# An attention kernel's normalised input: turned through DRAM and VectorE instead of TensorE, with a reordered opening

## What is computed

```python
x_norm = (x - mu) / jnp.sqrt(var + EPS) * gamma + beta
q = x_norm @ qkv[:, :KEY]
k = x_norm @ qkv[:, KEY:2 * KEY]
v = x_norm @ qkv[:, 2 * KEY:]
scores = jnp.einsum('bsk,btk->bst', q, k) * scale
scores = jnp.where(causal[None], scores, -jnp.inf)
out = jax.nn.softmax(scores, axis=-1) @ v
out = out @ o_proj
x1 = _layernorm(x + out + x)
...
h = jax.nn.silu(x1 @ w1.T); h = jax.nn.silu(h @ w3.T); h = h @ w2.T
out = out.at[indices_k[:, k]].add(gates[:, k:k + 1] * h)
```

## Time and profile before

| | |
|---|---|
| three runs | 1683.23, 1684.08, 1684.34 us (median 1684.08) |
| profiled execution, its time | 1682.32 us |
| span in the profile | 1680.3 us |
| granted TensorE clock, mean | 1.00 |
| TensorE busy (PE) | 98% of the span |
| VectorE (DVE), ScalarE (ACT), GpSimd (POOL) busy | 49%, 40%, 17% |
| DMA | 92.58 MB, mean 55 GB/s |

### The profile page before, as it was taken

How to read it: one execution, slowest core, us unless ns; L and a number is a source line. 1 busy time by engine, 2 the same in 40 slices (tenths; PEclk the granted TensorE clock), 3 DMA queues, 4 the chain that set the end, 5 groups by cost and what they waited for, 6 DMA issues and landing times.

```text
span 1680.3 us, 23574 instructions
## 1 busy us (share of the span) xinstructions
PE 1650.4 (98%) x7923; PEld 1369.7 (82%) x7923; DVE 828.1 (49%) x2168; ACT 671.6 (40%) x1301; POOL 282.6 (17%) x491
## 2 busy tenths in 40 slices
PE   7999999999999999999999999999999999999998
PEld 5888888878888888788888888888878888888886
DVE  5454434454453445455343456443456556555563
ACT  5443333443342334343322445332344444444443
POOL 1120201111120111121110112010122212212121
PEclk9999999999999999999999999999999999999999
DMA  4111201121111011121101132111154223132200
GB/s 157 57 51 51 70 32 38 64 71 63 70 51 51 32 50 64 58 101 49 53 19 38 45 100 95 38 57 45 63 115 74 36 39 50 25 50 43 32 0 7
DMA packets 173764, 92.58 MB, mean 55 GB/s; under 512 B 137296, under 2 KB 137296, under 8 KB 173664
## 3 DMA queue, kind: packets, MB, share of 16 engines
q1 hardware_dynamic: 162768, 72.41, 15.8%
q10 hardware_dynamic: 10896, 18.90, 3.6%
HBM read 57.71 MB, written 33.57 MB: 54 GB/s over the span
## 4 chain that ended last, share of the span: by engine, by line
PE 79%; issue 13%; POOL 3%; ACT 3%; DVE 2%; DMA 1%; SPq 0%; ACTq 0%; POOLq 0%; DVEq 0%
PE psum L334 24%; PE psum L336 24%; PE psum L335 24%; PE psum L1221 3%; PE psum L1159 1%; POOL rstd L454 1%; PE psum L1326 1%; PE psum L1325 1%; PE psum L1318 1%; PE psum L1317 1%; ACT xin L580 1%; ACT tok L580 1%; POOL expo L529 1%; ACT affine L564 0%; DVE stats L823 0%
## 5 line engine op out<-in xcount | busy, mean ns | idle before, releaser
L334 PE MATMUL psum<-xt_hi,g_hi 128*128 128x512 f32 (+3 forms) x640 | 239.5, 374 | 0.4 <-DVE g_lo L849 0.4
L628 ACT ACTIVATE pt_hi<-psum 128x512 fp32r<-128x512 f32 (+3 forms) x160 | 84.8, 530 | 369.6 <-PE psum L1221 363.7
L336 PE MATMUL psum<-xt_lo,g_hi 128*128 128x512 f32 (+3 forms) x640 | 230.0, 359 | 0.0
L335 PE MATMUL psum<-xt_hi,g_lo 128*128 128x512 f32 (+3 forms) x640 | 229.2, 358 | 0.0
L334 PE MATMUL psum<-v_hi,pt_hi 128*128 128x512 f32 x544 | 222.8, 410 | 1.8 <-DVE pt_lo L859 1.4
L336 PE MATMUL psum<-v_lo,pt_hi 128*128 128x512 f32 x544 | 213.1, 392 | 0.0
L335 PE MATMUL psum<-v_hi,pt_lo 128*128 128x512 f32 x544 | 212.8, 391 | 0.0
L451 POOL TENSOR_TENSOR var_eps<-meanvar,eps 128x2 f32<-128x2 f32 (+1 forms) x97 | 19.3, 199 | 1048.8 <-DVE meanvar L827 1046.7
L864 DVE TENSOR_REDUCE rowmax<-psum 128x1 f32<-128x512 f32 (+3 forms) x160 | 97.5, 610 | 197.7 <-PE psum L336 197.2
L746 ACT ACTIVATE act_f<-psum 128x512 f32<-128x512 f32 x128 | 76.5, 598 | 210.0 <-PE psum L336 210.0
L529 POOL TENSOR_TENSOR expo<-euler,shifted 128x32 f32<-128x32 f32 x16 | 86.9, 5430 | 298.0 <-DVE shifted L1061 298.0
(11 more groups left out here) (145 smaller groups left out, 3401.7 us busy)
## 6 DMA issues: line engine op xcount, KB each, us to landing
xin<-in_x ACTq DMA_DIRECT2D x64, 256.0 KB, 2.8
tok<-in_x SPq DMA_DIRECT2D x64, 256.0 KB, 2.6
x_scratch<-tok SPq DMA_DIRECT2D x64, 256.0 KB, 2.0
out_dram<-tok SPq DMA_DIRECT2D x64, 256.0 KB, 2.0
x_in<-x_scratch SPq DMA_DIRECT2D x64, 256.0 KB, 4.2
xin<-in_w_t ACTq DMA_DIRECT2D x8, 256.0 KB, 2.8
w_sb<-in_w_t SPq DMA_DIRECT2D x1, 1024.0 KB, 5.2
raw<-in_wq_t SPq DMA_DIRECT2D x1, 768.0 KB, 6.1
```

Source lines behind the costliest of these rows:

```text
L334: pe.matmul(o, ws, ms, start=first, stop=False, skip_group_check=True)
L335: pe.matmul(o, w_lo, ms, start=False, stop=False, skip_group_check=True)
L336: return pe.matmul(o, ws, m_lo_, start=False, stop=last, skip_group_check=True)
L628: act.activation(pt_hi[:, n % 2, 0:w], psum[:, turn_bank(turn_use(t, c)), 0:w], ACT.Copy).then_inc(pt_hi_ready, 1)
```

## The change

For all groups but the first of batch 0, TensorE no longer turns the input. SP stores each normalised pair of tiles in DRAM (`xn_scratch`) and reads a group back with quadrants exchanged (`load_xq`: 16 DMAs of 64 KB) into the place of `xt_lo`; VectorE transposes it in 32x32 blocks into the place of `xt_hi` (`turn_x`, four instructions of 128x512); ScalarE applies gamma and beta back into the place of `xt_lo` (`affine_x`); VectorE splits it there (`split_x`, now one feature chunk of all four tiles of the group, where a unit was two chunks of two tiles). Transposes of group g+1 stand in tile k = 1, with the statistics of a pair moved there from k = 0; splits 0 to 3 in tile k = 2. For group 0 of the next batch transposes and splits 0 and 1 stand at the end of tile 14, splits 2 and 3 in tile 15, which also gets a pair's statistics. SP, not ScalarE, now loads `xin`. Since a split covers all four tiles, the first `project_v` of a group waits for all four splits.

In the opening, TensorE runs 14 matmuls on a constant, starts the fold before the first turn, and leaves the last block of the second fold to the end; pairs 2 to 4 of batch 0 have buffers of their own.

```diff
+            def store_xn(b, pair, first=False):
+                sp.wait_ge(x_normed, b * PAIRS + pair + 1)
+                sp.dma_start(pair_rows(xn_scratch, b, pair), x_pair(pair, first)).then_inc(xn_stored, DMA)
+            def load_xq(b, g):
+                rows_of = xn_scratch[bass.ds(b * S + g * (GROUP * P), GROUP * P), :].rearrange("(t j) (c q i) -> q j c t i", j=LANES, q=QUADRANTS, i=LANES)
+                for c in range(DC):
+                    for q in range(QUADRANTS):
+                        sp.dma_start(xt_b[q * LANES:(q + 1) * LANES, c, columns(g)].rearrange("j (t i) -> j t i", i=LANES),
+                                     rows_of[q][:, c]).then_inc(xq_loaded[g % 2], DMA)
...
+                if t == TILES - 1 and not last:
+                    sp.wait_ge(scores_ready, b * CHUNKS + BEFORE[t] + 1)
+                    load_xq(b + 1, 0)
...
+            def affine_x(b, g, c):
+                act.wait_ge(xq_turned, (b * GROUPS + g - 1) * DC + c + 1)
+                act.activation(xt_b[:, c, columns(g)], xt_a[:, c, columns(g)],
+                               ACT.Identity, bias=beta_sb[:, c:c + 1], scale=gamma_sb[:, c:c + 1]).then_inc(affine_ready, 1)
...
+            def turn_x(b, g, c):
+                dve.wait_ge(xq_loaded[g % 2], (2 * b + (g + 1) // 2) * DC * LOADS)
+                dve.transpose(xt_a[:, c, columns(g)], xt_b[:, c, columns(g)]).then_inc(xq_turned, 1)
...
-                if more and k == 0:
+                if more and k == 1:
+                    for c in range(DC):
+                        turn_x(b, g + 1, c)
+                if more and k == 2:
+                    split_x(b, g + 1, 0)
                     split_x(b, g + 1, 1)
-                if more and k == 2:
-                    split_x(b, g + 1, 2)
...
+                if t == TILES - 2 and not last:
+                    for c in range(DC):
+                        turn_x(b + 1, 0, c)
+                    split_x(b + 1, 0, 0)
+                    split_x(b + 1, 0, 1)
                 if more and k == 2:
+                    split_x(b, g + 1, 2)
                     split_x(b, g + 1, 3)
                     split_v(b, GROUP * (g + 1))
                     split_g(b, g + 1)
...
+                if more and k == 1:
+                    affine_x(b, g + 1, 0)
+                    affine_x(b, g + 1, 1)
...
+                if tile % GROUP == 0 and tile:
+                    pe.wait_ge(xt_ready, 1 + (b * GROUPS + tile // GROUP + 1) * XUNITS)
...
-                if more and k == 2:
-                    turn_x(b, g + 1, 2)
-                if t == TILES - 2 and not last:
-                    turn_x(b + 1, 0, 0)
-                if t == TILES - 1 and not last:
-                    turn_x(b + 1, 0, 2)
...
+            for _ in range(WARMING):
+                pe.matmul(psum[:, XBANK, 0:P], ident[:], ident[:], start=True, stop=True)
+            fold_weights(0, 0, (0, 1))
+            turn_x(0)
+            fold_weights(0, 0, (2, 3))
+            turn_x(1)
+            for c in range(1, DC):
+                fold_weights(0, c, range(DC))
+            for c in range(2):
+                fold_weights(1, c, range(DC - 1))
+            turn_x(2)
+            for c in range(2, DC):
+                fold_weights(1, c, range(DC - 1))
+            turn_x(3)
+            for c in range(DC):
+                fold_weights(1, c, (DC - 1,))
```

More of the change, by code:

```diff
@@ L346, in load_x1, with x_pair, pair_rows, stored @@
                                  rows_of[q]).then_inc(x1_loaded[slot], DMA)
+        def x_pair(n, first):
+            if first and n in EARLY:
+                return xt_a[:, n - 1, 2 * GROUP * P:4 * GROUP * P].rearrange("p (s d) -> p s d", s=2)
+            return xin[:]
+        def pair_rows(dram, b, pair):
+            return dram[bass.ds(b * S + 2 * pair * P, 2 * P), :].rearrange("(s p) d -> p s d", p=P)
+        def stored(b, pair):
+            return (b * PAIRS + pair - 1) * DMA
+        def second_half(g):
+            return 2 * (g + 2) + 1
+        def first_half(g):
+            return 2 * (g + 3)
+        def ahead(b, pair, last):
+            if pair < PAIRS:
+                return b, pair
+            return None if last else (b + 1, pair - PAIRS)
+        def columns(g):
+            return slice(GROUP * g * P, GROUP * (g + 1) * P)
         block = whole.enter_context(nc.Block())
@@ L390, in tile @@
                     store_out(b - 1, TILES + t - 3)
-            for t in range(3):
-                tile(0, t, before=False)
+                if normed:
+                    sp.wait_ge(xn_stored, stored(*normed))
+                    to_load = ahead(b, first_half(g) if k else second_half(g), last)
+                    if to_load:
+                        load_x(*to_load)
+                if k == GROUP - 1:
+                    if g + 2 < GROUPS:
+                        sp.wait_ge(scores_ready, b * CHUNKS + 1)
+                        load_xq(b, g + 2)
+                    elif g + 2 > GROUPS and not last:
+                        sp.wait_ge(scores_ready, b * CHUNKS + BEFORE[t] + 2)
+                        load_xq(b + 1, g + 2 - GROUPS)
+            for t in range(2):
+                tile(0, t, before=False)
+            for n in EARLY[0:2]:
+                store_xn(0, n, first=True)
+            sp.wait_ge(xn_stored, stored(0, EARLY[1]))
+            load_xq(0, 1)
+            store_xn(0, EARLY[2], first=True)
+            tile(0, 2, before=False)
             with sp.Fori(0, B - 1) as b:
@@ L476, in tile @@
                 pool.tensor_tensor(y, y, y, ALU.add).then_inc(res_doubled, 1)
[L477 to L480, removed]
+                if k == GROUP - 1 and ahead(b, first_half(g), last):
+                    norm_x(*ahead(b, first_half(g), last))
                 if t:
@@ L484, in tile @@
                     norm_behind(b - 1, TILES - 1)
[L485 to L490 removed]
+                if t == 0 and not before:
+                    norm_x(b, EARLY[2])
+                if k == 1 and ahead(b, second_half(g), last):
+                    norm_x(*ahead(b, second_half(g), last))
             def batch(b, last):
@@ L497, in batch @@
                         tile(b + 1, t)
-            for pair in range(FIRST_PAIRS):
+            for pair in range(FIRST_PAIRS - 1):
                 norm_x(0, pair)
@@ L828, in statistics, with norm_x @@
                 done.then_inc(requested, 1)
[L830 to L839, removed]
+            def norm_x(b, pair, first=False):
+                if first and pair in EARLY:
+                    dve.wait_ge(x_early_loaded[pair - EARLY[0]], DMA)
+                else:
+                    dve.wait_ge(x_loaded, (pair + 1) * DMA if first else (b * PAIRS + pair - 2) * DMA)
+                if not first or pair:
+                    dve.wait_ge(x_normed, b * PAIRS + pair)
+                y = x_pair(pair, first)
+                statistics(lambda s: y[:, s - 2, :], 2, 4, x_variance)
@@ L934, in tile @@
                     split_v(b, t + 1)
-                if t == TILES - 2 and not last:
-                    split_x(b + 1, 0, 1)
                 if t == TILES - 1 and not last:
@@ L959, in tile @@
                         split_v(b, GROUP * (g + 1) + j)
-                if more and k == 0:
-                    norm_x(b, 2 * (g + 1) + 1)
-                if t == TILES - 2 and not last:
-                    norm_x(b + 1, 1)
+                if t == 0 and not before:
+                    norm_x(b, EARLY[2], first=True)
+                if k == 1 and ahead(b, second_half(g), last):
+                    norm_x(*ahead(b, second_half(g), last))
                 from_tile = TILES - 1 - GROUP
```

216 lines of the change are left out of this document (105 added, 111 removed).

## The result

The changed kernel takes 1714.71 us (median of 4 runs, 1712.17 to 1717.38) against 1683.78 us before (1683.23 to 1684.34): ratio 1.018, interval 1.0168 to 1.0192. It is 30.9 us slower; 12 were forecast, and the time lies 4.7 us above the upper end of the range. The profiled execution took 1712.17 us, its span 1710.4, 30.1 above the span before.

A forecast was written before the change was run, and what follows sets the result against it. TensorE, busy 98%, was taken as the bound, with VectorE's list order deciding its waits. 29.6 + 4.5 - 14.4 - 24.4 - 4.8 - 2.2 = -11.7 gave 1694.0 us profiled, 1696 against the median; range 1685 to 1710.

The forecast's parts named there:

- What is taken away: TensorE, main stage: 60 units of four transposes go at 0.44 us each; with the turns' waits, 29.6 us gained.
- The opening: Start of batch 0: constant's matmuls take the slow-clock time and the fold starts earlier; 4.5 us gained, bounds 2 and 6.7.
- Tile 6: Every k = 2: TensorE waits for VectorE's fourth split, also delayed from tile 5; 3.6 us, 14.4 in four batches.
- the clock: Rival: TensorE's clock falls in the new gaps, 2.1 us each; 1704, or 1713 with tile 6's gaps; chance 0.17.
- Tile 2: TensorE waits for VectorE's fourth split: 6.5 us three times, 5.0 in batch 0; together 24.4 us.
- Tile 10 and the ends of batches: Tile 10: 0.25 us a batch, within 2.2 of smaller costs; batch ends: VectorE's list delays tile 15's `pt_lo`, 4.8 in all.
- The rival of the late group: Next batch's group lands late if each of SP's 16 DMAs costs 1.43 us: 10 us three times, 1726; chance 0.10.
- VectorE in time: Rival: in tiles 2 and 6 the fourth split ends before TensorE arrives; 38.8 us of cost go, 1657; chance 0.08.

The follow-up runs named there:

- GpSimd held back: Changed kernel with GpSimd's doubling of the residual in tiles 3, 7 and 11 waiting for the fourth split: 1709.23 us.
- the gaps were filled: Changed kernel with 24 matmuls of the constant ahead of TensorE's wait for the splits in tile 2 and 9 in tile 6: 1703.49 us.
- a better order: The version one tile earlier, with two splits moved from tile 1 to 2, two from 14 to 15, GpSimd's doubling delayed in tiles 6 and 10: 1661.93 us.
- the version one tile earlier: Changed kernel with turns at the end of tiles 0, 4, 8 and ScalarE's passes and the splits in tiles 1, 5, 9: 1673.62 us.
- tile 2 filled: Changed kernel with thirty matmuls of the constant ahead of TensorE's wait for the splits in tile 2 of each batch: 1710.62 us.

## Why the prediction was wrong, point by point

- **What is taken away** held at 0.43 to 0.44 us a unit where nothing takes its place (tile 8 became 0.87 shorter, by two units). In tile 4 a wait of 0.55 to 0.69 for `pt_lo` took the place of the 0.54 for ScalarE, which the sum had booked as gained. Over tiles 0, 4 and 8 of four batches 2.4 us less were gained than forecast.
- **The opening** held: 4.2 for 4.5.
- **Tile 6** held. In order of time, the waits of TensorE there in batch 0:

```profile
132.74 0.47 PE L345 MATMUL psum<-v_hi,pt_hi 128*128 128x512 f32 x1 [0.63 <-DVE pt_lo L953]
...
140.20 0.50 PE L345 MATMUL psum<-wvo_hi,xt_hi 128*128 128x512 f32 x1 [2.42 <-DVE xt_lo L937]
...
143.05 0.39 PE L345 MATMUL psum<-xt_hi,m_hi 128*128 128x512 f32 x1
```

  The first is the delay from tile 5's transposes, the second the list behind the maximum; both were counted. Together 3.05 us of waits are listed. By the starts it is more: 12.2 less 1.6 for the clock, with 8 x 0.44 for the turns added again, is 14.1, 3.5 a batch for the 3.6 forecast. A listed wait is shorter than its delay, since matmuls stand 0.23 apart but their records last 0.39: 0.16 goes into the record ahead of the gap, and the pair behind it is some 0.1 wider (140.20 to 143.05 is 2.85, for 2.72 before).
- **Tile 2** held as far as VectorE's list goes: 33.5 less 9.7 for the clock and 3.5 for GpSimd is 20.3, forecast 20.9. The sum agrees better than its parts: with the turns added again the batches cost 4.9, 5.7, 5.8 and 7.3, for 5.0 and three times 6.5.
- **Tile 10 and the ends of batches.** Without GpSimd's 3.5 tile 10 would be at -1.2 for -1.3, and with GpSimd held back it measured -1.3. The batch ends cost 2.1 less than forecast, which happened to make up for tile 4: that is luck. (Some 0.5 of it is in the forecast's own sum, which has 2.3 us for four units and a wait; 4 x 0.44 and a third of 1.1 are 2.1.)
- **The failed step is the clock.** I held it as a rival with 0.17 beside the sum, when it was a term of the sum. The forecast put gaps of 5 to 6.5 us into tile 2 and counted them at no loss, though the trace was silent between 2.39 and 9.4 us and no row spoke for that. What the runs showed is a loss behind all four gaps of tile 2 and behind one of tile 6, 11.3 us in the profile, and 11.2 us regained in the times when the gaps were filled. The rival's price of 2.1 a gap was near: 2.1 to 2.6 in tile 2, 1.6 once in tile 6. The rule that I cited from the Trainium skill ("TensorE: Matmul & The Clock Gate", Why this matters for your kernels), that idle gaps between bursts bring the lower clock back, was right here: the trace agrees in all four gaps of 5.94 to 6.09 us.
- **The missing term** is GpSimd, which the prediction never looked at. Its doubling of the residual was in the trace of before, and was moved by nobody; VectorE's work was moved under it. Costed at nothing, it took 7.0 us in the trace; the times fell by 5.5 when it was held back, with the clock worse. Either of the two misses alone would have left the time inside the range: 1709.2 us with GpSimd held back, 1703.5 with the gaps filled.
- **The rival of the late group** fell: no transpose (L930) waited for a DMA, and SP issued a group's 16 in 8.84 us, not 23 (SP's queue in tile 3 of batch 1, beside the earlier trace rows):

```profile
388.74 8.84 SPq L434 DMA_DIRECT2D xt_b<-xn_scratch  x16
```

- **"VectorE in time"** fell for this change, but not for its idea. The 0.08 was right for the given order; 1657 was what it would be worth, and a better order reached 1661.9.

Without the clock and GpSimd the span would have grown by 30.1 - 11.3 - 7.0 = 11.8 us, and 11.7 were forecast. That the two agree so closely is owed in part to tile 4 and the batch ends, whose misses cancel; and no run had both causes taken out in the order of the changed kernel.

## What to carry to other kernels

Work that moves to an engine with half its time free is paid for at the place in that engine's list where somebody waits for its last item; count the list between the two, and move the items a tile earlier before giving the idea up. A gap of several microseconds on TensorE is priced with the slow matmuls that may follow it, as a part of the sum. And look at what the neighbour engine does in the very microsecond of the instruction that others wait for.

## What was not expected of the hardware

- The clock's fall is not a matter of the gap's length alone. Gaps of 4.56 us and more (four in the profile of the changed kernel, four in that of GpSimd held back) were all followed by matmuls 0.43 apart. Behind the same wait of 2.4 to 2.5 us in tile 6 it was one batch of four in the changed kernel, three with tile 2 filled, and four with GpSimd held back. In the version one tile earlier it did not fall behind 3.16 us in tile 2 of batch 0:

```profile
70.76:75.65 4.89, 4.89 (x22) 4.03 (x22) 2.94 (x10) 1.86 (x4) 1.87 (x5) 1.00 0.02 3
```

  What else decides was not tried.
- Plain element work of one engine on SBUF can hold up another's by most of its own length: 0.87 us for an overlap with 1.03. The one that starts first isn't always untouched: in the version one tile earlier, where the split started 0.36 us behind GpSimd's doubling, the split took 1.41 for 0.69 and the doubling 1.22 for 1.04.
